# Zeroing a scatter target in two parts, with the scatters let go range by range

## The reference

```python
dst = minimum((3125 * uniform(50000) ** 2).astype(int32), 99999)
order = argsort(dst); src, dst = src[order], dst[order]
# block 0, on the batch-normed features h
a_in  = segment_sum((h @ W_in + b_in)[src] * iw[:, None], dst, N)
a_out = segment_sum((h @ W_out + b_out)[dst] * ow[:, None], src, N)
# ... a gated update gives the new h; x = layernorm(x + h)
# blocks 1 to 3: segment sums over the same edges; block 1 also sums
# projected edge attributes (50000 x 64) at dst; degrees are counts at dst
```

## Time and profile before

| what | us |
|---|---|
| median of three runs | 3142.1 |
| the profiled execution's own time | 3144.16 |
| its span | 3142.4 |
| last slab issued, all slabs landed | 367.7, 389.3 |
| first one-hot of the edge loop | 317.5 |
| first and last scatter start | 389.5, 1155.5 |
| last one-hot done | 1131.1 |
| first load of the matrix stage | 1159.1 |

### The profile page before, as it was taken

One profiled execution on the slowest core, in us unless ns is written; L12 is line 12 of the kernel. 1 busy time (PEld: TensorE's weight loads), 2 busy tenths in 40 slices (PEclk: granted clock), 3 DMA queues, 4 the chain that ended last, 5 costly groups with the idle time before them and its releaser, 6 DMA issues.

```text
span 3142.4 us, 38353 instructions
## 1 busy us (share of the span) xinstructions
PE 2610.5 (83%) x15375; PEld 1439.8 (46%) x15375; DVE 1687.8 (54%) x1866; ACT 1264.6 (40%) x2580; POOL 822.5 (26%) x634
## 2 busy tenths in 40 slices
PE   0563888888888849899899799999999989899896
PEld 0421444444444425444444444565556655555543
DVE  4547999999999955555555453111122252223314
ACT  0113777777777736666666322011011121212203
POOL 3000078888887762222222000000000000000000
PEclk9776999999999979999999899999999999999897
DMA  9999822222222237777776533322322223332341
GB/s 372 402 381 402 344 19 18 15 19 18 19 15 19 15 70 260 243 238 236 233 241 209 147 74 107 109 78 98 107 84 92 85 87 128 109 115 95 96 147 61
DMA packets 210271, 440.30 MB, mean 140 GB/s; under 512 B 84427, under 2 KB 128700, under 8 KB 209862
## 3 DMA queue, kind: packets, MB, share of 16 engines
q1 hardware_dynamic: 134764, 408.55, 38.5%
q0 software_dynamic: 60768, 18.76, 6.8%
q10 hardware_dynamic: 14553, 10.47, 1.1%
HBM read 287.68 MB, written 150.02 MB: 139 GB/s over the span
## 4 chain that ended last, share of the span: by engine, by line
PE 49%; SPq 11%; POOL 11%; DVE 10%; DMA 7%; issue 6%; ACT 4%; DVEq 0%; ACTq 0%; POOLq 0%
PE psum L1079 25%; POOL cell_mat L535 11%; SPq L370 11%; PE psum L1027 11%; PE psum L959 6%; DVE AR L1405 4%; DMA cell_mat<-ROW 4%; ACT Q L673 3%; DVE Q L1450 2%; PE psum L973 2%; DMA Q<-cell_mat 1%; PE psum L1096 1%; ACT Q L664 1%; DMA cell_mat<-SA 1%; PE psum L1106 1%
## 5 line engine op out<-in xcount | busy, mean ns | idle before, releaser
L1079 PE MATMUL psum<-FR 125*128 125x500 f16 (+1 forms) x4200 | 822.7, 354 | 20.8 <-DVE FR L1504 20.8
L1405 DVE TENSOR_SCALAR AR<-Q,ROW 128x3125 f16<-128x3125 f16 x391 | 722.6, 1903 | 9.0 <-PE psum L916 1.8
L911 PE MATMUL psum<-AR,Q 128*128 128x500 f16 x2346 | 571.6, 379 | 138.9 <-DVE AR L1405 122.4
L535 POOL DMA_INDIRECT cell_mat<-ROW x391 | 617.2, 1578 | 159.6 <-issue 106.4
L1079 PEld LDWEIGHTS psum<-FR 125*128 125x128 f16 x4200 | 387.4, 98 | 429.5 <-issue 44.8
L1531 DVE SCALAR_TENSOR_TENSOR Q<-psum,small,ROW 128x1000 f32<-128x1000 f32 (+1 forms) x42 | 48.2, 1148 | 713.2 <-PE psum L1079 713.1
L911 PEld LDWEIGHTS psum<-AR,Q 128*128 128x128 f16 x2346 | 199.1, 98 | 361.7 <-DVE AR L1405 129.9
L1450 DVE SCALAR_TENSOR_TENSOR Q<-Q,small 125x1000 f16<-125x1000 f32 (+1 forms) x175 | 252.4, 1446 | 205.4 <-ACT Q L673 204.8
L1027 PE MATMUL psum<-wl,Q 128*125 128x256 f32 (+1 forms) x1100 | 286.8, 401 | 5.7 <-ACT Q L730 3.0
L673 ACT ACTIVATE Q<-Q,small 125x1000 f16<-125x1000 f32 (+1 forms) x175 | 262.0, 1497 | 60.7 <-DMA Q<-cell_mat 60.5
L973 PE MATMUL psum<-Q,FR 125*128 125x500 f16 (+1 forms) x1050 | 237.8, 365 | 55.9 <-DVE Q L1450 54.3
(11 more groups left out here) (291 smaller groups left out, 2757.8 us busy)
## 6 DMA issues: line engine op xcount, KB each, us to landing
cell_mat<-SA SPq DMA_DIRECT2D x39, 3000.0 KB, 32.3
Q<-cell_mat SPq DMA_DIRECT2D x150, 750.0 KB, 5.3
FR<-count_mat SPq DMA_DIRECT2D x180, 625.0 KB, 3.8
count_mat<-Q SPq DMA_DIRECT2D x150, 125.0 KB, 4.9
FR<-in_edge_attr POOLq DMA_DIRECT2D x13, 960.0 KB, 9.4
Q<-in_edge_attr SPq DMA_DIRECT2D x41, 256.0 KB, 2.7
cell_mat<-ROW POOLq DMA_INDIRECT x391
Q<-cell_mat SPq DMA_DIRECT2D x25, 187.5 KB, 2.8
```

Of the source, the lines that this page charges most:

```text
L535: pool.indirect_dma_start(out=cell_mat, out_offset=bass.IndirectOffsetOnAxis(ap=at[c % VALS][:, k:k + 1], axis=0), in_=vals[c % VALS][:, k ...
L911: pe.matmul(a, own_attr, onehot[t % 3][:, t0:t0 + nt], start=t == 0, stop=t == ET - 1, skip_group_check=True)
L1079: last = pe.matmul(a[:, hh, 0:w], parts[:, c, t, f], slot(m, j)[0:P, i_, :], start=t == 0 and c == 0, stop=t == NT - 1 and c == 1, skip_gr ...
L1405: dve.tensor_scalar(onehot[t % 3], iota16, dst_c[:, t:t + 1], None, ALU.is_equal).then_inc(S["onehot_ready"], 1)
```

## The change

Four things change.

1. The order of edges. Tile t now holds 128 edges out of 1024 that are neighbours in the sorted list, so its targets lie close together. To get that, SP loads the four edge lists as 48 rows of 1024, and TensorE turns them with 32 small transposes into the old place. The attribute chunks are read in the same order (`attr_chunk`).
2. Zeroing in two parts. SP zeroes range 0 after the input and raw weights have landed, then waits until 12 of the 14 attribute reads for the maximum are done (`peak_read`), then issues the rest. Afterwards it counts the ranges that have landed (`ranges_zeroed`). GpSimd works out how far each of seven groups of 56 tiles reaches (`need`) and waits only for that count.
3. Three of the maxima over the attributes are taken ahead of the input mean, and the maxima of the features are mixed in with the others.
4. ScalarE copies tile t + 1 of the projection before it waits for tile t, from eight buffers instead of four; and it issues the loads of attribute chunks 2 to 13, which GpSimd issued before for chunks 0 to 6.

```diff
+        LAST_ZERO = 2
+        DUMP = -(-(3 * (N * N + 2 * N) // SLAB * SLAB + 128 * ZERO * LAST_ZERO) // 3)
-    EARLY = 7
+    EARLY = 14
+    PEAKS_EARLY = 3
+    FULL = EM // EC
+    REACH = 7
+    RT = -(-ET // REACH)
+    FEATURES_AFTER = {4: 0, 6: 1, 8: 2, 10: 3, 12: 4}
...
         def _(sp):
+            for i, b in enumerate((src, dst, edge_w, edge_w2)):
+                rows_i = edge_ints[...] if i < 2 else edge_rows[...]
+                sp.dma_start(rows_i, b[0:FULL * 128 * EC].rearrange("(c e) -> c e", c=FULL)).then_inc(S["edges_in"], 16)
...
             sp.wait_ge(S["zeros"], 1)
-            for j in range(3 * CELLS // SLAB):
-                sp.dma_start(flat_cells[j * SLAB:(j + 1) * SLAB]..., zero_block...).then_inc(S["zeroed"], 16)
+            sp.wait_ge(S["x_in"], 32)
+            sp.wait_ge(S["raw_in"], 16 * 4 * LAYERS)
+            sp.dma_start(flat_cells[3 * DUMP:3 * DUMP + 3 * 512]...).then_inc(zero_in[0], 16)
+            slabs = [0] * NR
+            for j in range(3 * DUMP // SLAB + 1):
+                k = REPEAT if j < 3 * DUMP // SLAB else LAST_ZERO
+                g = min(r for r in range(NR) if j * SLAB < 3 * N * COLS * (r + 1) or r == NR - 1)
+                slabs[g] += 1
+                if g == 1 and slabs[g] == 1:
+                    sp.wait_ge(S["peak_read"], PEAK_LOADS - 1)
+                sp.dma_start(flat_cells[j * SLAB:j * SLAB + 128 * ZERO * k]..., zero_block...).then_inc(zero_in[g], 16)
+            for r in range(NR):
+                sp.wait_ge(zero_in[r], 16 * (slabs[r] + (r == 0)))
+                sp.sem_inc(S["ranges_zeroed"], 1)
...
         def _(pool):
-            for i in range(2):
+            for i in range(2 + PEAKS_EARLY):
+                if i >= 2:
+                    pool.wait_ge(S["peak_read"], i - 1)
                 load_peaks(i)
...
-            pool.wait_ge(S["zeroed"], 16 * (3 * CELLS // SLAB))
+            pool.wait_ge(S["reach_ready"], 1)
+            ranges_needed = [pool.value_load(need[0:1, i:i + 1], min_val=1, max_val=NR) for i in range(REACH)]
             for t in range(ET):
+                if t % RT == 0:
+                    pool.wait_ge(S["ranges_zeroed"], ranges_needed[t // RT])
+                    pool.sem_inc(S["let_go"], 1)
+                    pool.wait_ge(S["let_go"], t // RT + 1)
...
         def _(act):
+                if k == 0 and c + 2 < EARLY:
+                    act.wait_ge(S["attr_lo"], c + 1)
+                    act.dma_start(attr32[c % 2], attr_chunk(c + 2)).then_inc(attr_in[c % 2], 16)
...
         def _(pe):
+            for i in range(4):
+                for k in range(EC):
+                    last = pe.transpose(psum[:, i, k * FULL:(k + 1) * FULL], edge_rows...[:, i, :, k], ident[0:FULL, 0:FULL])
...
         def _(dve):
+            for i in range(REACH):
+                last = dve.tensor_reduce(reach[:, i:i + 1], cell_less[:, i * RT:min((i + 1) * RT, ET)], AX.X, ALU.max)
...
+            for i in range(PEAKS_EARLY):
+                attr_peak(i)
             dve.wait_ge(S["out_done"], 1)
...
+            for i in range(PEAKS_EARLY, PEAK_LOADS + 1):
+                attr_peak(i)
+                if i in FEATURES_AFTER:
+                    feature_peaks(FEATURES_AFTER[i])
```

More of the change, by code:

```diff
@@ L227, in build_gnn @@
         w_e1, w_e2, src_f = (Q[:, qe + i * ETP:qe + (i + 1) * ETP] for i in range(2, 5))
+        edge_rows = AR[0:FULL, 2000:2000 + 4 * 128 * EC]
+        edge_ints = edge_rows[:, 0:2 * 128 * EC].bitcast(I32)
+        turned_edges = lambda i: psum[:, i, 0:EC * FULL].rearrange("p (k c) -> p c k", k=EC)
+        tile_order = lambda v: v[:, 0:FULL * EC].rearrange("p (c k) -> p c k", k=EC)
+        reach, reach_top = FR[:, 5100:5100 + REACH], FR[0:REACH, 5120:5121]
         iota_f = FR[:, 0:N]
@@ L290, in build_gnn @@
         S = {n: sem(n) for n in names}
-        hT_out = [sem(f"hT_out{s}") for s in range(4)]
+        hT_out = [sem(f"hT_out{s}") for s in range(8)]
         peak_in = [sem(f"peak_in{s}") for s in range(2)]
+        zero_in = [sem(f"zero_in{r}") for r in range(NR)]
         attr_in = [sem(f"attr_in{s}") for s in range(2)]
@@ L405, in load_epilogue @@
                 sp.dma_start(hT_now[r % 2][:, :, 0:nt * P], hT_d[:, :, t0 * P:(t0 + nt) * P].rearrange("h p n -> p h n")).then_inc(epi_in[r % 2], 16)
-            for s in range(4):
-                sp.wait_ge(hT_out[s], 16 * len(range(s, NT, 4)))
+            for s in range(8):
+                sp.wait_ge(hT_out[s], 16 * len(range(s, NT, 8)))
             for s in range(4):
@@ L515, in _ @@
                 pool.dma_start(by_node(h_d)[lo:hi], Xn[lo:hi]).then_inc(S["h_kept"], 16)
-            for i in range(2, PEAK_LOADS):
+            for i in range(2 + PEAKS_EARLY, PEAK_LOADS):
                 pool.wait_ge(S["peak_read"], i - 1)
@@ L572, in keep @@
                 act.wait_ge(S["tr_read"], TR_AT["feat", t])
[L573 to L578, removed]
-                if t:
[L580 to L584, removed]
+                act.dma_start(hT_d[:, :, t * P:(t + 1) * P].rearrange("h p n -> p h n"), hT(t)).then_inc(hT_out[t % 8], 16)
+            for t in range(NT + 1):
+                if t < NT:
+                    act.wait_ge(S["tr_done"], TR_AT["feat", t])
+                    if t >= 8:
+                        act.wait_ge(hT_out[t % 8], 16 * (t // 8))
+                    act.activation(hT(t), trp[:, t % 2, 0:2 * P].rearrange("p (h n) -> p h n", h=2), ACT.Copy).then_inc(S["tr_read"], 1)
+                if t:
+                    u = t - 1
+                    keep(u)
+                    act.wait_ge(S["out_done"], OUT_AT["feat", u])
+                    act.activation(Bn[0][:, u], outp(u)[:, 0:D], ACT.Copy).then_inc(S["nat_ready"], 1)
+                    act.activation(Bn[1][:, u], outp(u)[:, D:2 * D], ACT.Copy).then_inc(S["out_read"], 1)
             act.wait_ge(S["scale0_ready"], 1)
@@ L592, in _ @@
                     act.wait_ge(S["peak_read"], PEAK_LOADS + 1)
+                    for s in range(8):
+                        act.wait_ge(hT_out[s], 16 * len(range(s, NT, 8)))
                 act.activation(feat[b][:, now, 0], Bn[b][:, now], ACT.Copy, scale=scale0[0:P, 0:1]).then_inc(S["feat_hi"], 1)
@@ L612, in attr_hi @@
             def attr_hi(c):
-                if c < EARLY:
-                    act.wait_ge(early_in[c % 2], 16 * (c // 2 + 1))
+                if c < 2:
+                    act.wait_ge(early_in[c], 16)
                 else:
-                    act.wait_ge(attr_in[c % 2], 16 * len(range(EARLY + (c - EARLY) % 2, c + 1, 2)) + (16 if c == CH - 1 else 0))
+                    act.wait_ge(attr_in[c % 2], 16 * (c // 2) + (16 if c == CH - 1 else 0))
                 if c >= 2:
@@ L635, in _ @@
             act.wait_ge(S["feat_split"], 2 * PIECES)
-            for s in range(4):
-                act.wait_ge(hT_out[s], 16 * len(range(s, NT, 4)))
             attr_hi(0)
@@ L655, in _ @@
             act.wait_ge(S["attr_done"], ET)
+            act.wait_ge(S["ranges_zeroed"], NR)
             act.activation(SA[:, 0:4 * COLS].rearrange("p (b n) -> p b n", b=4), psum[:, 0:4, 0:COLS], ACT.Copy, scale=unscale_a).then_inc(S["s_ready"], 1)
@@ L811, in _ @@
             pe.wait_ge(S["masks"], 5)
+            pe.wait_ge(S["edges_in"], 16 * 12)
+            pe.wait_ge(S["edge_step"], 1)
+            for i in range(4):
+                for k in range(EC):
+                    last = pe.transpose(psum[:, i, k * FULL:(k + 1) * FULL], edge_rows.rearrange("c (i p k) -> c i p k", i=4, k=EC)[:, i, :, k], ident[0:FULL, 0:FULL])
+            last.then_inc(S["edges_turned"], 1)
             pe.wait_ge(S["cell_ready"], 1)
+            pe.transpose(psum[0:REACH, 7, 0:128], reach, ident[:, :])
             for b in range(4):
@@ L1216, in _ @@
             link(dve.memset(weights[:, :, 0], 1.0))
-            dve.wait_ge(S["edges_in"], 128)
+            dve.wait_ge(S["edges_in"], 16 * 12)
             dve.wait_ge(S["masks"], 1)
             main, tail = (slice(0, 128), slice(0, EM)), (slice(0, TAIL), slice(EM, ET))
-            for s in (main, tail):
+            dve.tensor_copy(edge_rows[:, 0:2 * 128 * EC], edge_ints).then_inc(S["edge_step"], 1)
+            for s in ((slice(0, 128), slice(FULL * EC, EM)), tail):
                 dve.tensor_copy(src_f[s], src_i[s])
-                last = dve.tensor_copy(dst_c[s], dst_i[s])
+                dve.tensor_copy(dst_c[s], dst_i[s])
+            dve.wait_ge(S["edges_turned"], 1)
+            for i, v in enumerate((src_f, dst_c, w_e1, w_e2)):
+                last = dve.tensor_copy(tile_order(v), turned_edges(i))
             link(last)
@@ L1229, in _ @@
             link(dve.tensor_tensor(cell_less, cell_less, dump, ALU.add))
+            for i in range(REACH):
+                last = dve.tensor_reduce(reach[:, i:i + 1], cell_less[:, i * RT:min((i + 1) * RT, ET)], AX.X, ALU.max)
+            link(last)
```

(1 more changed line is left out.)

40 lines of the change are left out of this document (27 added, 13 removed).

## The result

The change makes the kernel slower. The median of four runs is 3183.7 us (3183.14 to 3185.99), against 3144.4 us (3141.87 to 3146.78) for the kernel before on the same chip. The ratio is 1.0127, 95% interval 1.0115 to 1.0140. The forecast was 3157 us, so direction and range held, but the loss is 39.3 us and not 14.8.

A forecast was written before the change was run, and what follows sets the result against it. Bound: first scatter plus 391 scatters at GpSimd's own pace. Terms +20.5 (later first scatter), +6.3, -8.4, -5.7 and +2.1 gave +14.8 us on the 3142.1 median, so 3157 us; 8 in 10 range 3136 to 3188.

The forecast's parts named there:

- The bound: Edge loop: its end is the first scatter plus 391 scatters at GpSimd's own pace, 1.945 us each; VectorE then waits 130 us.
- The order on SP: Zeroing: SP raises the range count only behind its last slab's issue, so no scatter starts before that, near 410 us.
- rival A: Edge loop: scatters really go range by range, the first at 254 us, following VectorE; time 3052 us, chance 0.06.
- The front part: Before the edge loop: norming starts at 73.9 us, projection at 118.6, first feature maximum at 134.7, one-hots at 227.
- T12: Time when 12 attribute reads are done and the second part of the zeroing begins; forecast 186 us.
- The second part of the zeroing: SP's remaining 31 slabs and a third, at 7.37 then 7.93 us each, end at 431 us; first scatter at 410.
- the sum: Start of the scatters: the forecast's terms added up to a first scatter at 410 us, 20.5 us later than before.
- The credit of 21.6 us: End of the zeroing: slabs still queued when SP gets free, so the first scatter comes 21.6 us before the zeroing ends.
- The small terms: Edge loop: scatters beside last slabs +6.3 us, no waits for values -8.4, last 70 tiles -5.7, range-count waits +2.1.
- B: Edge loop: scatters to neighbouring columns land half a us slower, most then wait; +61 us, 3218 us, chance 0.08.
- C: Edge loop or front part: neighbouring targets remove 44 landing waits, 19.6 us, or T12 is about 172; 3137 us, chance 0.14.
- Rival D: Projection: every tile takes the first tile's 5.4 us, so T12 is about 222; +36 us, 3193 us, chance 0.10.

## Why the forecast had the direction and not the size

**The bound.** Right: first scatter plus GpSimd's own pace, with VectorE waiting at the end. From first scatter to first matrix load it took 761.5 us; the forecast had 1174 - 410 = 764.

**The order on SP.** Right: the counts stand behind all issues, so rival A didn't happen by itself. The experiment that made it happen came out at 3107 us and not at A's 3052. A let the scatters follow VectorE from the start and forgot what beside slabs each one costs.

**The front part.** Nearly right: norming at 75.1 (73.9), projection at 119.7 (118.6), first maximum at 134.5 (134.7). The load behind the store, 24.2 us to landing instead of the 9.6 assumed for any load, was not foreseen; the store was in the change's order and I priced only the loads. The trace of the kernel before had it to read: the two loads issued behind the same store, at 148.3 and 152.4 us, landed 35.0 and 34.8 us later, and the 9.6 us come from a load with no store ahead of it. T12 was 194.1 instead of 186, the first one-hot 234.7 instead of 227.

**The second part of the zeroing. This is the step that failed, by its size.** It said that the zeroing ends at 431 us and the first scatter comes 21.6 us ahead of that. The last slab landed at 452.9 us, 258.9 us behind T12 and not 245, and the scatter came 16.3 us ahead of that. So the first scatter, at 436.65 us, was late by 8.1 (T12) + 13.9 + 5.3 = 27.3 us against the sum, which gave 409.4 before it was rounded to 410. The forecast lacked 24.5 us in all; the other terms together came out some 3 us too high. Two parts of the 13.9 us show in the stages: the last 17.9 us ran at 174 GB/s, worth (405 - 174) x 17.9 / 405 = 10.2 us, and the restart's 41 us at 385 GB/s, 2.0. The intervals of 7.37 and 7.93 us were taken between issues in a full stretch, and a stretch that starts and drains takes longer. Also, a slab of 3.07 MB in 7.37 us is 417 GB/s, more than any stage of the two kernels moved. The credit of 21.6 us was measured where 249 GB/s were moved in that time, 5.4 MB; here 3.1 MB were left when SP got free.

The view that I didn't use would have been simpler: add up the bytes that must move before SP is free, 144 to 146 MB here, and ask in which stretches the engines are given fewer than they can take. By that the hold costs 53 us, the late start 13, the restart 2 and the 2 MB more that were moved by then 5. Against that stand 6 us of slack that the kernel before had between 140 and 285 us, and 21 us won because the first scatter follows SP's last issue and not the last landing. That makes 46, and the first scatter moved by 47.1. From it to the first matrix load it took 761.5 us instead of 769.6, most of it because the 11.1 us of waits for values are gone. So 39 us are left, as measured. Nor could the 8.1 us of T12 be had back by moving the store: T12 then stood where the forecast had it, and SP was free only 2.2 us earlier.

**The small terms.** Scatters beside the last slabs cost (453.53 - 436.65) - 5 x 1.945 = 7.2 us, forecast 6.3. Waits for values went as forecast. At the end 80 scatters ran at 1.86 us beside an idle VectorE, where the forecast had 70 at 1.863. Rivals B and C (other landings with sorted targets) fall: 36.6 us in 38 waits for landings, against 32.8 in 44. Rival D falls: behind the first tile the next eight began 2.15 us apart. Its own T12 of 222 was too low, since 20 tiles of 5.4 us alone end at 118.6 + 108 = 226.6.

The Trainium skill (DMA: Bandwidth & Descriptors, section Specifications) gives some 358 GB/s as a core's HBM limit, half of the 716 GB/s of a stack that two cores share. By that figure the 144 MB of the kernel before would need an estimated 402 us. The trace doesn't agree: they were moved in 367.7, and the changed kernel ran at 405 GB/s for 200 us on end. One core ran here; no run shows the rate with a second one busy. So the sums above go by the measured rate.

## What to carry to other kernels

Before transfers are held back to clear the way for others, add up bytes times rate by stage: a hold pays only if the transfers that it lets through fill the engines, and every stretch that it leaves half idle comes back at the end if the rest waits for the last of the transfers, as here. Look where a "ready" count is raised, too: a count behind blocking issues on the same engine is no finer than one wait for everything, and moving it into the loop was worth some 76 us with the hold and 43 without it. What then starts early runs beside the transfers at half its pace, so shorten that stretch as well.

## What the hardware showed that I had not expected

- An adding scatter of 128 cells with two in flight runs at 1.94 us behind the slabs, 1.86 us beside an idle VectorE, and 3.90 us beside 3 MB slabs.
- After SP's last slab issue the DMA engines moved only 161 to 263 GB/s for some 17 to 22 us, in every run whose stages were read.
- After a pause SP issued three slabs in 4.17 us and was then held for some 8 us by each, on the mean.
- A 960 KB load issued near 124 us landed 24.2 us later behind a store of 3.2 MB on GpSimd's queue, and 5.1 us later with the store moved behind the loads.
